# Heads times gated output weights: from one full float32 product to two rounded products on stacked halves

## The reference, cut to what matters

```python
ga = (2 * (ga >= 0) - 1) * jnp.maximum(jnp.abs(ga), 0.25)      # a gate per sequence and feature
h = _layernorm(x, axis=-1) * (1 + ca) + sa
# inside the attention, per step: h = o_t * Cq / denom          (64 numbers per token)
# out = h_in + jnp.einsum('btd,md->btm', h, Wout)               Wout is 128 x 64
x = x + ga * attention(h)                                       # so: x + ga*h_in + heads @ (Wout.T * ga)
# then a second layer norm and the experts:
h = jax.nn.relu(jnp.einsum('th,ehf->etf', xf, W1) + b1[:, None, :])
y = jnp.einsum('etf,efh->eth', h, W2) + b2[:, None, :]
```

## Time and profile before

| | |
|---|---|
| median of the runs | 343.36 us (341.14, 343.36, 343.36) |
| profiled execution, whole | 340.84 us |
| its span, first to last instruction | 338.8 us |
| PE | 94% of the span busy, 1700 records |
| DVE | 82%, 798 |
| POOL | 51%, 173 |
| ACT | 48%, 300 |
| chain of work that ended last | PE 80%, DVE 8%, DMA 4%, ACT 4% |
| mean granted TensorE clock | 0.985 of full speed |

### The profile page before, as it was taken

The page is one execution under the profiler, slowest core; times in us unless marked ns, Lnnn a source line. Parts: engine busy times, 40 slices in busy tenths (PEclk is TensorE's granted clock), DMA queues, the critical chain, the costliest instruction groups (busy, mean ns, idle before and its releaser), DMA issues.

```text
span 338.8 us, 4962 instructions
## 1 busy us (share of the span) xinstructions
PE 318.0 (94%) x1700; PEld 255.6 (75%) x1700; DVE 278.7 (82%) x798; ACT 164.0 (48%) x300; POOL 171.5 (51%) x173
## 2 busy tenths in 40 slices
PE   1989977999999999999999999999999999998995
PEld 1978974888687877888687868786888778776883
DVE  5486676799879996999699987999679969987774
ACT  1262434265464736555537545473655554345442
POOL 6720370258554783378526864488326842435340
PEclk9999996799999999999999999999999999999999
DMA  5860004200071004300170006100520025005301
GB/s 131 247 192 2 2 0 133 118 4 0 1 250 31 3 0 170 112 0 1 47 236 2 0 3 250 31 0 0 188 96 2 0 72 210 1 1 160 123 0 31
DMA packets 13726, 24.13 MB, mean 71 GB/s; under 512 B 1779, under 2 KB 8102, under 8 KB 12678
## 3 DMA queue, kind: packets, MB, share of 16 engines
q1 hardware_dynamic: 13474, 23.70, 21.2%
q10 hardware_dynamic: 164, 0.07, 0.1%
q0 software_dynamic: 64, 0.07, 0.1%
HBM read 21.60 MB, written 2.23 MB: 70 GB/s over the span
## 4 chain that ended last, share of the span: by engine, by line
PE 80%; DVE 8%; DMA 4%; ACT 4%; issue 2%; POOL 1%; SPq 1%; DVEq 0%; POOLq 0%
PE bank L1038 9%; PE bank L1039 8%; PE bank L1040 8%; PE bank L1050 8%; PE bank L1060 8%; PE bank L1051 8%; PE bank L993 6%; PE bank L978 3%; PE bank L926 3%; PE bank L941 2%; DMA gate_bc<-gates_d 2%; PE bank L1077 2%; PE bank L1083 2%; PE bank L1000 2%; DMA wmod_sb<-in_L_wmod_dram 1%
## 5 line engine op out<-in xcount | busy, mean ns | idle before, releaser
L453 POOL TENSOR_TENSOR hg_lo<-hg,hg_hi 128x512 fp32r<-128x512 f32 x65 | 87.5, 1355 | 74.0 <-ACT hg_hi L507 74.0
L507 ACT ACTIVATE hg_hi<-hg 128x512 fp32r<-128x512 f32 x128 | 79.8, 628 | 80.0 <-DVE hg L815 78.7
L815 DVE SCALAR_TENSOR_TENSOR hg<-bank,neg_b,gate_bc 128x512 f32<-128x512 f32 x128 | 94.3, 742 | 23.7 <-DMA gate_bc<-gates_d 14.8
L1038 PE MATMUL bank<-h_hi,w_hi 128*128 128x512 f32 x128 | 58.7, 459 | 1.5 <-ACT gate_rows L545 1.5
L1039 PE MATMUL bank<-h_hi,w_lo 128*128 128x512 f32 x128 | 51.2, 400 | 0.0
L1040 PE MATMUL bank<-h_lo,w_hi 128*128 128x512 f32 x128 | 51.2, 400 | 0.0
L1050 PE MATMUL bank<-hg_hi,w_hi 128*128 128x512 f32 x128 | 50.8, 397 | 0.0
L1060 PE MATMUL bank<-hg_lo,w_hi 128*128 128x512 f32 x128 | 50.6, 396 | 0.0
L1051 PE MATMUL bank<-hg_hi,w_lo 128*128 128x512 f32 x128 | 50.2, 392 | 0.0
L828 DVE TENSOR_TENSOR hg_lo<-hg,hg_hi 128x512 fp32r<-128x512 f32 x63 | 47.1, 747 | 1.1 <-ACT hg_hi L507 0.6
L422 POOL TENSOR_SCALAR var_eps<-mv 128x4 f32<-128x4 f32 x16 | 4.9, 305 | 72.5 <-DVE mv L579 72.5
(11 more groups left out here) (160 smaller groups left out, 545.5 us busy)
## 6 DMA issues: line engine op xcount, KB each, us to landing
gate_bc<-gates_d SPq DMA_DIRECT2D x8, 1024.0 KB, 6.9
gate_bc<-gates_d SPq DMA_DIRECT2D x16, 256.0 KB, 3.6
gate_bc<-gates_d SPq DMA_DIRECT2D x8, 512.0 KB, 4.9
out_dram<-x_all SPq DMA_DIRECT2D x8, 256.0 KB, 2.3
w_raw<-in_L_ffn_W_dram SPq DMA_DIRECT2D x1, 1024.0 KB, 9.0
x_all<-in_L_attn_x_dram SPq DMA_DIRECT2D x2, 256.0 KB, 4.3
wmod_sb<-in_L_wmod_dram SPq DMA_DIRECT2D x1, 384.0 KB, 5.0
gates_d<-gate_rows SPq DMA_DIRECT2D x8, 16.0 KB
```

The lines of the kernel that those rows point to most:

```text
L453: g.tensor_tensor(hg_lo[k][:, :], hg[k][:, :], hg_hi[k][:, :].bitcast(fp32), ALU.subtract).then_inc(s_lo_pool, 1)
L507: a.activation(hg_hi[k][:, :], hg[k][:, :], ACT.Copy).then_inc(s_hghi, 1)
L815: v.scalar_tensor_tensor(hg[k][:, :], up_bank[n % 4][:, :], neg_b1[:, n:n + 1], gate_bc[own % 2][:, n // NU, :], ALU.max, ALU.mult).then_i ...
L1038: t_.matmul(dst, w_hi, hx, start=True, stop=False)
```

## The change

The product heads x gated weights is made of rounded parts. hhT now has 128 partitions of type fp32r: ACT writes the rounded heads into the first 64 (as before, but rounding), and DVE writes what the rounding left into the other 64 (a new instruction at the start of turn 5, new semaphore s_hhlo). Wout is loaded twice, side by side, so that its transpose, woutT and wout_ga have their 64 rows twice, on 128 partitions. ACT rounds wout_ga to wg_hi (128 partitions x 1024, body -2, t = 13), POOL subtracts for wg_lo (64 partitions x 1024, body -1, t = 3). For each of the four tiles PE now makes two products instead of the one: all 128 rows of hhT with wg_hi, which is high x high plus low x high, and the first 64 rows with wg_lo, which is high x low.

```diff
-        wout_raw = sb("wout_raw", [D, DH])
+        wout_raw = sb("wout_raw", [D, 2 * DH])
-        woutT = sb("woutT", [DH, D])
+        woutT = sb("woutT", [2 * DH, D])
-        wout_ga = sb("wout_ga", [DH, B, D])
+        wout_ga = sb("wout_ga", [2 * DH, B, D])
+        wg_hi = sb("wg_hi", [2 * DH, B, D], fp32r)
+        wg_lo = sb("wg_lo", [DH, B, D], fp32r)
-        hhT = sb("hhT", [DH, T])
+        hhT = sb("hhT", [2 * DH, T], fp32r)
...
-            sp.dma_start(wout_raw[:, :], Wout).then_inc(s_wqko, 16)
+            for h in range(2):
+                sp.dma_start(wout_raw[:, h * DH:(h + 1) * DH], Wout).then_inc(s_wqko, 16)
...
+                    if opening and t == LAG:
+
+                        pool.wait_ge(s_wghi, 1)
+                        g.tensor_tensor(wg_lo[:, :, :], wout_ga[0:DH, :, :], wg_hi[0:DH, :, :].bitcast(fp32),
+                                        ALU.subtract).then_inc(s_wglo, 1)
...
+                    if weights_hi and t == 13:
+                        act.wait_ge(s_wga, 2)
+                        a.activation(wg_hi[:, :, :], wout_ga[:, :, :], ACT.Copy).then_inc(s_wghi, 1)
                     if t == 4 and end:
                         act.wait_ge(s_hhT, m1 + 1)
-                        a.activation(hhT[:, :], bB[0:DH, :], ACT.Copy).then_inc(s_hhc, 1)
+                        a.activation(hhT[0:DH, :], bB[0:DH, :], ACT.Copy).then_inc(s_hhc, 1)
...
-            v.tensor_copy(woutT[:, :], bank[3][0:DH, 0:D]).then_inc(s_proj, 1)
+            v.tensor_copy(woutT[:, :], bank[3][:, 0:D]).then_inc(s_proj, 1)
...
                     v.scalar_tensor_tensor(wout_ga[:, 4 * n:4 * n + 4, :],
-                                           bank[n][0:DH, :].rearrange("p (b d) -> p b d", b=4), 0.5,
-                                           woutT[:, :].unsqueeze(1).to_broadcast([DH, 4, D]),
+                                           bank[n][:, :].rearrange("p (b d) -> p b d", b=4), 0.5,
+                                           woutT[:, :].unsqueeze(1).to_broadcast([2 * DH, 4, D]),
                                            ALU.mult, ALU.mult).then_inc(s_wga, 1)
...
                 for t in range(LAG, N + LAG):
+                    if t == 5 and end:
+
+                        dve.wait_ge(s_hhc, m1 + 1)
+                        v.tensor_tensor(hhT[DH:2 * DH, :], bB[0:DH, :], hhT[0:DH, :].bitcast(fp32), ALU.subtract).then_inc(s_hhlo, 1)
...
-            pe.wait_ge(s_wqko, 48)
+            pe.wait_ge(s_wqko, 64)
...
-                        wait_apart(pe, s_hhc, m1 + 1)
-                        wg = wout_ga[:, :, :].rearrange("p b d -> p (b d)")[:, bass.ds(m1 * D, D)]
+                        wait_apart(pe, s_hhlo, m1 + 1)
+                        pe.wait_ge(s_wglo, 1)
                         for j in range(NT):
-                            last = t_.matmul(bC[:, j * P:(j + 1) * P], hhT[:, j * P:(j + 1) * P], wg, start=False, stop=j == NT - 1,
+                            c = slice(j * P, (j + 1) * P)
+                            t_.matmul(bC[:, c], hhT[:, c], wg_hi[:, m1, :], start=False, stop=False, skip_group_check=True)
+                            last = t_.matmul(bC[:, c], hhT[0:DH, c], wg_lo[:, m1, :], start=False, stop=j == NT - 1,
                                              skip_group_check=True)
                         last.then_inc(s_x1p, 1)
...
-                    if opening and t == 5:
-                        pe.wait_ge(s_wga, 2)
```

More of the change, by code:

```diff
@@ L266, in adaln_mlstm_moe_kernel @@
         s_hhc = sem("s_hhc")
+        s_hhlo = sem("s_hhlo")
+        s_wghi = sem("s_wghi")
+        s_wglo = sem("s_wglo")
         s_x1p = sem("s_x1p")
@@ L885, in _ @@
             t_.transpose(bank[2][:, 0:2 * DH], vo_raw[:, :], ident[:, :])
-            t_.transpose(bank[3][0:DH, 0:D], wout_raw[:, :], ident[:, :]).then_inc(s_wT, 1)
+            t_.transpose(bank[3][:, 0:D], wout_raw[:, :], ident[:, :]).then_inc(s_wT, 1)
             pe.wait_ge(s_silu, 1)
```

## The result

| | before | changed |
|---|---|---|
| median of four runs | 343.36 us (341.14 to 344.38) | 352.06 us (348.59 to 353.32) |
| profiled execution, whole | 340.84 us | 348.59 us |
| its span | 338.8 us | 347.1 us |
| mean granted clock in it | 0.985 | 0.985 |
| one steady period, mean of five | 36.5 us | 37.4 us |

The changed kernel is slower: a ratio of 1.026 with a 95% interval of 1.018 to 1.034 (a fifth run of it took 353.54 us). The prediction was 350.5 us, 345 to 354.5, by a stall at every switch between 128 and 64 rows of weights. In this and all later tables the medians are of all runs, while the ratios are estimated from the fast runs alone (those within some 1.5% of the kernel's fastest), so the two can differ by some tenths of a per cent.

A forecast was written before the change was run, and what follows sets the result against it. PE's queue was taken to bound the steady part, with DVE close behind. Terms of 5.5 + 0.5 + 1.6 + 0.55 + 0.25 = 8.4 us gave 349.2 to 351.8 us, forecast 350.5 us, range 345 to 354.5.

The forecast's parts named there:

- The block: PE's changed products: eight row-count switches make eight records of 0.26 us each, +0.79 us per steady block, +5.5 in seven.
- The reading that L978 enters in the same way: PE's load for L978, with 1 weight row, also waits for the product under way: 88.29, where L1060 started at 87.89.
- Rival 1: Switching rows in PE's blocks is free: loads 0.11 us apart, -1.2 us in all, 342.1 us against the median; chance 0.17.
- rival 2: Only one direction of row switch stalls in PE's blocks: 3.7 us in all, 347.0 us against the median; chance 0.13.
- The wait in turn 5: PE waits for DVE's subtraction instead of ACT's copy: about +0.1 us in each of five steady blocks, +0.5 us.
- Block 7: Last steady block: DVE has no statistics there and is early, so no new wait, only the +0.79 us of the products.
- The opening: Opening block: subtraction behind two w_lo subtractions +0.58 us, eight records of 0.26 us +0.99, together +1.6 us.
- +0.55 us for the second load of Wout: Setup: one more DMA issue on SP ahead of wmod, on the chain, costs 0.55 us.
- +0.25 us for ACT's rounding: Setup: ACT's rounding of wout_ga ends at 27.1, delaying exponentials that could start at 26.89, by 0.25 us.
- the first exponential: Sign in the setup on ACT: the first exponential should come 0.8 us later than 26.9.
- The sum: Whole kernel: 5.5 + 0.5 + 1.6 + 0.55 + 0.25 = 8.4 us slower.
- The level: Whole time: 349.2 us from the profiled execution or 351.8 from the median; level unknown, so 350.5 in between.

The follow-up runs named there:

- e4: Changed kernel with its products reordered so that the weight-row count switches four times per block instead of eight: 347.11 us in one run.
- e1: Changed kernel with each block's four 128-row products first, then the four 64-row ones (two switches): 342.62 us, 1.003 of the kernel before.
- e2: Changed kernel with the second product of each tile also taking 128 rows (no switches): 340.32 us, 0.998 of the kernel before.
- e5: Changed kernel with DVE's subtraction for the low heads moved ahead of the statistics: span 345.1 us in its profile.
- e3: Kernel before with its float32 heads and gated weights padded with zeros to 128 rows: 340.46 us, 0.997 of the kernel before.
- e7: Zero-padded (128-row) kernel before plus thirteen small unread products filling PE's waits in the opening: 336.13 us, 0.984 of the kernel before.

## Why the prediction was right, and where it was off

**The block.** Right, as a mechanism and in size: eight records of 0.26 us predicted, 0.255 measured, because of the eight switches of the row count. e4, e1 and e2 take away four, six and eight of them and leave eight products, and the block falls by 0.144 us for each. The reading that L978 enters in the same way was loose: its load starts at 88.29, 0.17 us after L1060's stream ends and not 0.09, and no run touched it, so a single row of weights is not covered by what is shown.

**Rival 1, free switches.** Wrong. What spoke for it was the page "TensorE: Matmul & The Clock Gate" of the Trainium skill, section "LDWEIGHTS (loading the stationary operand)", by which the rows don't matter. That holds for a load's duration (0.19 us with 128 rows, 0.18 with 64 in the trace above), and says nothing of when it can start. The runs decide: 2.04 us for eight products with the switches, 0.89 us without. (In rival 2's sum the opening's 1.1 us should have been 0.58 + 4 x 0.37 - 1.09 = 0.97.)

**The wait in turn 5.** About 0.1 us predicted in five blocks, 0.16 to 0.19 measured: the steps were 0.92 to 0.95 us where block 6, which has no wait, as predicted, has 0.76, and e5 gave 0.16 to 0.2 back. Block 7 was mis-sized: I took DVE to be early there. It is idle, but ACT's copy ends only at 294.7, since in that body PE has no transposes of xn between the heads and the next products. The low heads are there at 295.4, and PE's first load at 295.48 is 0.62 us behind the one before. A wait that moves from ACT to an engine behind ACT has to be placed by the end of ACT's work too.

**The opening.** +1.6 us predicted and measured: the subtraction stands behind the two w_lo (34.29 + 1.26 = 35.55), ends at 36.27, PE loads at 36.32, and the block takes 2.04 us.

**Setup.** The +0.55 us for the second load of Wout was wrong. wmod's issue moved from 3.00 to 3.56, but it landed 4.1 us after its issue instead of 5.0, and its first product started at 7.82 us, 0.3 us earlier than the 8.11 of before. Over the twelve traces that product starts at 7.32 to 8.13 us in the eight with both loads and at 7.77 to 8.11 in the four with one: the later issue cannot be seen in it. The +0.25 us for ACT's rounding came nearly as predicted: ACT ends it at 26.57, its next exponential starts at 26.47 (the two overlap in the records), 0.21 us after mb was done at 26.26, where before that took 0.04. But the first exponential, for which 0.8 us later than 26.9 was the sign, came 0.45 us earlier, because mb itself was ready 0.6 us earlier. In the twelve traces mb starts at 25.21 to 26.54 us, with either number of loads, so the -0.5 us of this pair lies within what the setup varies from run to run.

**The sum.** 8.3 us measured and 8.4 predicted is closer than the terms deserve, and that part is luck. The setup was 1.3 us too high; the waits of blocks 1 to 5 (0.2), block 7 (0.2) and two places without any term (0.7) were too low by about as much. The blocks themselves, 6.5 of the 8.4 us, are what was understood.

**The level.** I said that I didn't know at which level the changed kernel would sit, and took the middle. The two levels are the clock's dip. With the same mean clock the sum is 8.3 us against 8.4 predicted; the median of 352.06 lies 1.6 us above my number because all of its runs but the profiled one had clocks of 0.972 to 0.978. Against the median of before, the sum gave 351.8.

## What to carry to other kernels

Keep the number of weight rows the same along a stream of short products, or sort the products by it: each switch between 64 and 128 rows cost 0.144 us here, and 0.20 behind a product that streams longer than a load takes, more than a whole product of 128 columns (0.11 us); padding with zero rows added nothing to a block. When a wait is moved from one engine to the next, place it by the end of the slowest thing in that chain in every body of the program, and ask what each displaced instruction will then lie beside. Where runs of one kernel spread, read their mean clock before their medians.

## What the runs showed that I had not expected

The low clock in the opening cost more than the products could have gained (2.9 us, rival 1): thirteen products that nobody reads took the median of the kernel before from 343.41 to 338.25 us, and its spread in four runs to 0.8 us. With the padding of e3 the fastest kernel, e7, stands at 336.13 us, against 342.59 for the kernel before beside it. And DVE's subtraction of 128 x 512 took 1.32 us beside POOL's norm instead of 0.68.
